# Both sparse layers of a small transformer: norm, router, top two and slots in one block instead of three or four, and attention heads without padding

## The reference

```python
# L1_ffn: 8 experts, two per token
h = (x - mu) * rsqrt(var + 1e-5) * ln_g + ln_b
logits = einsum('btd,ed->bte', h, w_r) + b_r
topk_vals, topk_idx = top_k(logits, 2)
gates = softmax(topk_vals)
mixed = sum(experts(h)[topk_idx] * gates)          # gelu FFN, 128 -> 512 -> 128
# L2_ffn: 8 heads of 16 features
x = x + depthwise_conv3(x) + pos_b
q, k, v = split(x @ qkv_w.T + qkv_b)
idx = top_k(q . k * 128**-0.5, 16);  out = softmax over those 16, times v;  out @ wo_w.T + wo_b
# L3_ffn: 16 experts, two per token, and a shared one
gate_probs = softmax(xf @ gate_w + gate_b);  w, idx = top_k(gate_probs, 2);  w = w / sum(w)
# every expert: swiglu with clamps softplus(raw), scale a[1], shift a[2], then @ expert_w2 + b2
```

## Time and profile before

| what | value |
|---|---|
| median of 3 runs | 1469.47 us (1467.23 to 1474.43) |
| the profiled execution, its own time | 1468.95 us |
| its span in the trace | 1467.1 us |
| busy share PE, DVE, ACT, POOL | 77%, 79%, 45%, 45% |
| first sparse layer, norm to slots | 367.2 to 399.6 us |
| top-16 attention | 621.7 to 1248.4 us |
| state-space block | 1260.4 to 1287.5 us |
| second sparse layer, norm to slots | 1287.8 to 1329.4 us |
| its experts | 1329.7 us to the end |

### The profile page before, as it was taken

How to read it: one execution, slowest core, us unless ns; L and a number is a source line. 1 busy time by engine, 2 the same in 40 slices (tenths; PEclk the granted TensorE clock), 3 DMA queues, 4 the chain that set the end, 5 groups by cost and what they waited for, 6 DMA issues and landing times. The chain is left out here.

```text
span 1467.1 us, 29812 instructions
## 1 busy us (share of the span) xinstructions
PE 1128.4 (77%) x10536; PEld 794.0 (54%) x10544; DVE 1153.9 (79%) x2165; ACT 656.7 (45%) x1184; POOL 656.4 (45%) x569
## 2 busy tenths in 40 slices
PE   5877989998599987888777777777777775758771
PEld 3735566665489966645444444444444444547660
DVE  4676766562625599689999999999999996757994
ACT  4253434342125422156556555655565553013771
POOL 2033324240275762235555555555555554215344
PEclk9899999999689999999999999999999998879995
DMA  4090000000248710000000000000000000003882
GB/s 136 1 269 2 2 2 3 2 2 2 67 135 230 205 37 1 1 1 1 1 0 0 0 0 0 0 0 0 0 0 0 0 1 0 1 7 93 246 248 76
DMA packets 83386, 65.01 MB, mean 44 GB/s; under 512 B 13946, under 2 KB 73748, under 8 KB 83028
## 3 DMA queue, kind: packets, MB, share of 16 engines
q1 hardware_dynamic: 62868, 46.86, 11.4%
q0 software_dynamic: 4096, 8.40, 2.1%
q10 hardware_dynamic: 16320, 8.40, 1.9%
HBM read 43.70 MB, written 22.28 MB: 45 GB/s over the span
## 5 line engine op out<-in xcount | busy, mean ns | idle before, releaser
L1202 POOL TENSOR_TENSOR ta_ex<-ta_ex,ta_left 128x1024 f32<-128x1024 f32 x128 | 301.4, 2355 | 261.1 <-DVE ta_left L1251 261.1
L1071 PE MATMUL ta_ps_t<-consts,ta_ex 128*128 128x128 f32 x1024 | 141.3, 282 | 152.5 <-POOL ta_ex L1202 149.2
L1021 PE MATMUL ta_ps_s<-ta_kT,ta_qz 128*128 (+1 forms) x512 | 245.4, 603 | 0.5 <-ACT ta_ex L1129 0.5
L1071 PEld LDWEIGHTS ta_ps_t<-consts,ta_ex 128*128 128x128 f32 x1024 | 111.4, 142 | 239.0 <-POOL ta_ex L1202 214.3
L1235 DVE MAX8 ta_top<-ta_ps_s 128x8 f32<-128x1024 f32 x128 | 155.9, 1218 | 3.7 <-PE ta_ps_s L1021 3.7
L1241 DVE MATCH_REPLACE8 ta_left<-ta_etop,ta_ex 128x1024 f32<-128x1024 f32 x128 | 154.7, 1209 | 0.0
L1246 DVE MAX8 ta_second<-ta_left 128x8 f32<-128x1024 f32 x128 | 154.7, 1209 | 0.0
L1251 DVE MATCH_REPLACE8 ta_left<-ta_second,ta_left 128x1024 f32<-128x1024 f32 x128 | 154.7, 1208 | 0.0
L1129 ACT ACTIVATE ta_ex<-ta_ps_s,ta_ntop 128x1024 f32<-128x1024 f32 x128 | 140.2, 1096 | 0.0
L1021 PEld LDWEIGHTS ta_ps_s<-ta_kT,ta_qz 128*128 128x128 f32 x512 | 88.9, 192 | 70.5 <-issue 66.8
L2973 ACT ACTIVATE l1h_score<-l1h_work 128x2048 f32<-128x2048 f32 (+1 forms) x40 | 68.5, 1712 | 102.6 <-PE l1h_work L2780 102.5
...
...
## 6 DMA issues: line engine op xcount, KB each, us to landing
...
```

What stands on the lines that cost most here:

```text
L1021: ins = pe.matmul(ps_s[:, i % 2, half * BANK:(half + 1) * BANK], qz[:, odd, h, :], kT[:, grp, bass.ds(at.key0[i // PAIR] + half * BANK, BA ...
L1071: ins = pe.transpose(ps_t[:, j * P:(j + 1) * P], ex[:, i % 4, j * P:(j + 1) * P], m.ident)
L1202: pool.tensor_tensor(ex[:, i % 4, :], ex[:, i % 4, :], left[:, i % 4, :], ALU.subtract).then_inc(kept, 1)
```

## The change

In both sparse layers `routed_norm` takes the place of norm, router and slots: one block, no meeting of the engines inside it. Logits are made group by group (four tiles) into four PSUM banks, between the transposes, whose spins are gone. DVE reads them there: `max` gives a tile's eight largest, `max_index` their positions; the two picks are made from the index (`number` against `m.firsts`), the softmax of two from the difference of the top two values (`gap`), one Exp and a reciprocal. The products of picks with shares (`part`, `r.gates`, `r.scaled`) go to POOL. The rank matrix `later` is `before` minus one, so that the tile's own total need not be subtracted; the scan reads its totals from PSUM, and the rounding takes two operations instead of three. A spin of four matmuls stands ahead of the counting matmuls.

The owner tables (`below`, `owner`) move into the experts' blocks: in the first layer ahead of DVE's first work there, with SP's weight loads and POOL's staging waiting for `owned`; in the second between the first and second `clip`. There the table `par` is split in the shared expert's column (`par_s`, at the start) and the others (`par`, copied at pair 3, from matmuls that PE runs after pair 1 into the bank `ps_x[:, 0]`); the bias matmuls use one bank instead of two; the shares are reduced by DVE after the second `clip`.

The expert scalars move to the beginning of the state-space block (DVE and ACT), and the second layer's parameter DMAs move from its norm to the norm ahead of the state-space block. In the attention the padding is gone: q and k are one group of 128 rows, `m.eighth` masks a head of 16 rows, 4 first and 4 late projections instead of 8 and 8.

PE in the second sparse layer, before: the last rows of the norm, then the router, then the slots (`l3r_ps_l` are the logits, `l3k_ps_t` and `l3k_ps_r` the counts, an UNCONDITIONAL_BRANCH the end or start of a block).

The diff, cut to its core:

```diff
+def routed_norm(nc, m, r, name, E, blocks, wrT, src, dst, dstT, twice=False, fetch=None, gain=None, shift=None, scale=None, warm=0):
...
+            for g in range(TILES // 4):
+                dve.wait_ge(logits, g + 1)
+                for t in range(4 * g, 4 * g + 4):
+                    ins = dve.max(top[:, t, :], banks[g][:, (t % 4) * E:(t % 4 + 1) * E])
+                ins.then_inc(topped, 1)
+                dve.wait_ge(topped, g + 1)
+                for t in range(4 * g, 4 * g + 4):
+                    ins = dve.max_index(index[:, t, :], top[:, t, :], banks[g][:, (t % 4) * E:(t % 4 + 1) * E])
+                ins.then_inc(indexed, 1)
+            dve.wait_ge(indexed, TILES // 4)
+            dve.tensor_scalar(number[:, :, :], index[:, :, 0:2].rearrange("p t k -> p k t"), float(P), None, ALU.mult).then_inc(numbered, 1)
+            dve.tensor_tensor(gap[:, :], top[:, :, 1], top[:, :, 0], ALU.subtract).then_inc(gap_ready, 1)
+            dve.wait_ge(numbered, 1)
+            for k in range(2):
+                dve.tensor_tensor(r.picks[:, k, :, :], ...firsts..., ...number[:, k, :]..., ALU.is_equal).then_inc(picked, 1)
+            dve.wait_ge(picked, 2)
+            dve.tensor_tensor(kept[:, :, :, :], by_expert[0], by_expert[1], ALU.add).then_inc(kept_ready, 1)
+            dve.wait_ge(gap_exp, 1)
...
+            dve.tensor_tensor_scan(flat, again..., ps_t[:, 0:TILES * E], 0.0, ALU.mult, ALU.add).then_inc(step, 1)
+            dve.tensor_scalar(size[:, :, :], cum[:, :, :, CH - 1], (P - 1) / 2.0, CEIL, ALU.add, ALU.add).then_inc(step, 1)
+            dve.tensor_scalar(size[:, :, :], size[:, :, :], CEIL, None, ALU.subtract).then_inc(step, 1)
+            dve.tensor_tensor_scan(r.end..., again_e..., size..., 0.0, ALU.mult, ALU.add).then_inc(step, 1)
+            dve.tensor_tensor(first[:, :, :], r.end[:, :, :], size[:, :, :], ALU.subtract).then_inc(step, 1)
+            dve.tensor_tensor(cum..., cum..., first..., ALU.add).then_inc(step, 1)
+            dve.tensor_tensor(rank..., cum[:, :, :, :], ps_r..., ALU.add).then_inc(step, 1)
+            for k in range(2):
+                ins = dve.tensor_tensor(where[:, k, :, :], r.picks[:, k, :, :], rank[:, :, :], ALU.mult)
+            dve.tensor_reduce(slot[:, :, :], where[:, :, :, :], AX.X, ALU.add).then_inc(step, 1)
+            dve.tensor_copy(r.slot[:, :, :], slot[:, :, :])
 
         @block.gpsimd
+            pool.wait_ge(shared, 1)
+            for k in range(2):
+                pool.tensor_tensor(part[:, k, :, :], r.picks[:, k, :, :], shares[:, k, :]..., ALU.mult).then_inc(weighed, 1)
+            pool.tensor_tensor(r.gates[:, :, 0:E], part[:, 0, :, :], part[:, 1, :, :], ALU.add)
+            if scale is not None:
+                pool.tensor_tensor(r.scaled..., part..., scale..., ALU.mult)
 
         @block.tensor
             spin(pe, m, ps[:, 3, :], 8)
+            for g in range(TILES // 4):
+                for t in range(4 * g, 4 * g + 4):
+                    pe.wait_ge(normed, t + 1)
+                    ins = pe.transpose(ps[:, g, (t % 4) * P:(t % 4 + 1) * P], dst[:, t, :], m.ident)
+                ins.then_inc(turned, 1)
+                if g >= 1:
+                    score(g - 1)
+            score(TILES // 4 - 1)
+            spin(pe, m, ps[:, 0, :], 4)
+            pe.wait_ge(kept_ready, 1)
+            pe.matmul(ps_t[:, 0:TILES * E], m.one, kept..., start=True, stop=True).then_inc(ranked, 1)
+            pe.matmul(ps_r[:, 0:TILES * E], m.later, kept..., start=True, stop=True).then_inc(ranked, 1)
+            spin(pe, m, ps[:, 1, :], warm)
...
 def ssm_run  (@block.vector, ahead of the four jobs; ACT runs Exp, Ln and a priming Exp)
+            dve.scalar_tensor_tensor(size, raw, -1.0, raw, ALU.mult, ALU.max).then_inc(par_step, 1)
+            dve.wait_ge(par_exp, 2)
+            dve.scalar_tensor_tensor(clamp, raw, 0.0, soft, ALU.max, ALU.add).then_inc(par_step, 1)
...
+            dve.tensor_copy(x.wide[:, :, :], one[:, :].unsqueeze(2).broadcast_to([G, 6, L3_I]))
...
 def l3_experts  (@block.tensor)
+                if j == 1:
+                    pe.wait_ge(hot_step, 1)
+                    limits(ps_x[:, 0, :], hot[:, :], COLS)
 (@block.vector)
             clip(0)
+            dve.tensor_tensor(below..., r.end..., m.firsts..., ALU.is_le).then_inc(own_step, 1)
+            dve.tensor_reduce(owner[:, :, :], below[:, :, :, :], AX.X, ALU.add).then_inc(own_step, 1)
...
             clip(1)
+            dve.tensor_reduce(share[:, :, :], r.scaled[:, :, :, :], AX.X, ALU.add).then_inc(share_step, 1)
             for j in range(PAIRS):
+                if j == 3:
+                    dve.wait_ge(par_ready, 2)
+                    dve.tensor_copy(par..., ps_x[0:L3_I, 0, 0:7 * COLS]).then_inc(par_in, 1)
...
 def topk_attend
-            for k in range(4, 8):
-                pe.wait_ge(proj_done, k - 3)
-                project_first(k)
```

More of the change, by code:

```diff
@@ L850, in stage_l1_ffn @@
         r.gates = sb("gates", [P, TILES, 8])
-        r.picks, r.share = sb("picks", [P, 2, TILES, 8]), sb("share", [P, 2, TILES])
+        r.picks, r.shares = sb("picks", [P, 2, TILES, 8]), sb("shares", [P, 2, TILES])
+        r.end = sb("end", [P, B, 8])
         r.slot, r.owner = sb("slot", [P, 2, TILES], I32), sb("owner", [P, B, L1_BLOCKS], I32)
@@ L1404, in stage_l3_ffn @@
         r.hT, r.gates = m.xnT, sb("gates", [P, TILES, G])
-        r.picks, r.share = sb("picks", [P, 2, TILES, L3_E]), sb("share", [P, 2, TILES])
-        r.slot, r.owner = sb("slot", [P, 2, TILES], I32), sb("owner", [P, B, L3_BLOCKS], I32)
+        r.picks, r.shares, r.scaled = sb("picks", [P, 2, TILES, L3_E]), sb("shares", [P, 2, TILES]), sb("scaled", [P, 2, TILES, L3_E])
+        r.slot, r.end, r.hot_s = sb("slot", [P, 2, TILES], I32), sb("end", [P, B, L3_E]), sb("hot_s", [G, 1])
         r.gate_w, r.b_r = sb("gate_w", [P, L3_E]), sb("b_r", [1, L3_E])
@@ new lines, in _ @@
+            dve.wait_ge(picked, 2)
+            by_expert = [r.picks[:, k, :, :].rearrange("p (b t) e -> p b e t", b=B) for k in range(2)]
+            dve.tensor_tensor(kept[:, :, :, :], by_expert[0], by_expert[1], ALU.add).then_inc(kept_ready, 1)
+            dve.wait_ge(gap_exp, 1)
+            dve.tensor_scalar(shares[:, 0, :], gap[:, :], 1.0, None, ALU.add).then_inc(summed, 1)
+            dve.wait_ge(summed, 1)
+            dve.reciprocal(shares[:, 0, :], shares[:, 0, :]).then_inc(summed, 1)
@@ new lines, in _ @@
+            dve.wait_ge(summed, 2)
+            dve.tensor_tensor(shares[:, 1, :], gap[:, :], shares[:, 0, :], ALU.mult).then_inc(shared, 1)
+            if twice:
+                for k, of in enumerate(halves):
+                    dve.tensor_tensor(r.lift[:, 1, of], mean[:, of], rates[:, k, 1, :], ALU.mult)
+                    dve.tensor_scalar(r.lift[:, 0, of], rates[:, k, 1, :], 1.0, None, ALU.add)
+            dve.wait_ge(resets, 4)
+            dve.wait_ge(ranked, 1)
+            dve.nop(nofuse=True)
@@ L2014, in _, with score @@
-            for t in range(TILES):
-                pe.wait_ge(normed, t + 1)
-                ins = pe.transpose(ps[:, t // 4, (t % 4) * P:(t % 4 + 1) * P], r.hn[:, t, :], m.ident)
-                if t % 4 == 3:
-                    ins.then_inc(turned, 1)
-                    if t < TILES - 4:
-                        spin(pe, m, ps[:, 3, :], 1)
+            def score(g):
+                pe.matmul(banks[g][:, 0:4 * E].rearrange("p (t e) -> p t e", e=E), m.one[0:1, :],
+                          r.b_r[:, :].unsqueeze(1).broadcast_to([1, 4, E]), start=True, stop=False)
+                pe.wait_ge(hT_in, g + 1)
+                for t in range(4 * g, 4 * g + 4):
+                    ins = pe.matmul(banks[g][:, (t % 4) * E:(t % 4 + 1) * E], dstT[:, t * P:(t + 1) * P], wrT, start=False, stop=(t % 4 == 3))
+                ins.then_inc(logits, 1)
@@ L2022, in _ @@
+            pe.wait_ge(kept_ready, 1)
+            pe.matmul(ps_t[:, 0:TILES * E], m.one, kept[:, :, :, :].rearrange("p b e t -> p (b e t)"), start=True, stop=True).then_inc(ranked, 1)
+            pe.matmul(ps_r[:, 0:TILES * E], m.later, kept[:, :, :, :].rearrange("p b e t -> p (b e t)"), start=True, stop=True).then_inc(ranked, 1)
+            spin(pe, m, ps[:, 1, :], warm)
         @block.scalar
@@ L2079, in l1_experts_l2_attn @@
         prime = sb("prime", [P, 1])
+        below, owner = sb("below", [P, B, NB, E]), sb("owner", [P, B, NB])
         rows_dram = r.rows_dram
```

508 lines of the change are left out of this document (208 added, 300 removed).

## The result

| | before | changed |
|---|---|---|
| median | 1469.63 us (4 runs, 1467.23 to 1474.43) | 1456.35 us (4 runs, 1452.56 to 1459.37) |
| profiled execution (span) | 1468.95 us (1467.1) | 1459.37 us (1457.6) |
| mean granted clock of PE | 0.943 | 0.934 |

The ratio is 0.9895, 95% interval 0.9867 to 0.9923: faster by 13.3 us, where 24 were forecast. 1456.35 lies outside the range of 1440 to 1452. Among the experiments' executions two ran much slower at a low mean clock (one of e5's, 1544.73 us at .73, and one of before's, 1512.15 us at .82), and the ratios and e5's median leave them out. Each entry is the start of one instruction after less its start before; the step is the difference to the entry above.

What follows compares the result with a forecast made beforehand. Norm to slots in both sparse layers was taken as a chain of PE, DVE and ACT taking turns. Terms -8.3 - 2.8 + 1.3 - 14.5 + .5 = -23.8 from 1468.95 gave 1445.15, hence 1445.5 us; range 1440 to 1452.

Steps and rivals of the forecast that it cites:

- Experts of layer 2: Second sparse layer's experts: added owner, table, share-reduction and limit work mostly fits idle time; net +.5 us, bounds -.5 to +3.5.
- Rival B: Granted clock stays low at layer 2's spins (+1.5), attention startup (+1) and state-space back-projection (+1); 1449 us, chance .20.
- The last sign of the prediction: If blocks shorten as said but the total does not, the gain is handed back in the experts, by weights or bank.
- Rival W: Experiments' rival: work added to the shared expert's pairs makes them slow whatever the clock, 1456 us each time; no chance given.
- C: Second layer's experts pay all: limits, single bias bank, share reduction and copy uncovered, +3.5 for +.5; 1448.5 us, chance .15.
- Layer 1, -8.3: First sparse layer, norm to slots: slots there at 391.3 instead of 399.58, -8.3 us.
- Top-16 start, -2.8: Start of top-16 attention: four projections go behind the startup and DVE's first idle shrinks, -2.8 us.
- State space, +1.3: State-space block: expert scalars ahead of job 0 delay z by 1.1; +1.3 us, bounds 0 and +3.1.
- Layer 2, -14.5: Second sparse layer, norm to slots: block ends at 1314.9 instead of 1329.39, -14.5 us; alternatives -13.0 and -16.5.
- The race of spins and DVE: End of layer 2's slots: PE's last spin and DVE's cast end within .5 us of one another.
- Rival E: MAX and MAX_INDEX in both sparse layers cost the same on few elements; at 1.22 each 1507 us, chance .03.
- rival D: More gained: last scores at full clock, DVE not blocked so spins end earlier (-1.5), startup -3.1; 1441 us, chance .12.

Runs made afterwards that it cites:

- e5: e2 with 12 spins instead of 8 at the head of the second sparse layer's norm: median 1450.29 us, ratio .9855 to the kernel before.
- e2: Changed kernel plus four spins in PE's wait ahead of the first expert pair's down: median 1452.62 us, ratio .9875 to the kernel before.
- e1: The changed kernel run again without any edit: median 1455.14 us, ratio .9905 to the kernel before.
- e7: e2 with all expert scalars but the first operation moved ahead of the state-space block's last addition: median 1451.55 us, ratio .9876 to the kernel before.
- e10: The edits of e2, e5 and e7 together: median 1449.41 us, ratio .9847 to the kernel before.
- e3: Changed kernel with layer 2's owner table, limits and copies back ahead of the first clip, two bias banks: median 1457.52 us, ratio .9914 to the kernel before.
- e9: Kernel before with only the changed top-16 attention functions and mask: median 1470.00 us, ratio .9996 to the kernel before.
- e4: Changed kernel without the 14 spins at the end of the second layer's slots: median 1460.64 us, ratio .9935 to the kernel before.
- e6: e2 with POOL's products held until DVE's last operation of the slots: 1464.19 us in its one run.
- e8: e2 without the 4 spins ahead of the counting matmuls in both sparse layers: median 1456.68 us, ratio .9905 to the kernel before.
- e11: Changed kernel without the one spin ahead of each up of pairs 3 to 9: median 1456.38 us, ratio .9906 to the kernel before.
- e12: e10 without the one spin ahead of each up of pairs 3 to 9: median 1452.88 us, ratio .988 to the kernel before.

## Why the prediction was wrong

The step that failed is "Experts of layer 2: net +.5, bounds -.5 to +3.5". It priced instructions, in durations that the earlier trace rows and the pairs of before show at a granted clock of 1.00, and its upper bound assumed only that all of them lie uncovered. The stretch from clip 0 to 13 took 8.2 us more instead of 1.0. The instructions cost 1.08 of it (e2, full clock). The clock cost 7.1 more in the first profile and 3.9 in e1's (clip 0 to 13, less e2's). Rival B named the clock, but put it at the spins, the attention's start and the back-projection, and at 3.5 us in sum; no term had the pairs in it, where PE is 100% busy and every matmul counts twice when the clock is halved. The last sign of the prediction came true, the gain was handed back in the experts, but neither by weights nor by a bank. Rival W, my C, is refuted as the cause: with its work in place the pairs are fast when the clock is full (39.4 us in e2, e5, e7 and e10), and with its work taken out the kernel is no faster (e3).

This one step does not explain the whole miss. The median lies 10.9 us over the forecast, and e2, whose profile has the pairs at the full clock, is 17.9 us faster than its before, where 24 were forecast; 1452.62 would still have been just outside the range. The rest is spread over the steps below, and how much the medians owe to the pairs' clock is known only as the 2.5 us between e1 and e2, within overlapping intervals.

By the other steps:

- Layer 1, -8.3: measured -7.4 (6.6 to 8.9 over ten profiles). The order of events was right; the spins at .50 were sized .9 too short.
- Top-16 start, -2.8: the place gained 3.4, of which 2.65 was a wait for ACT that the prediction did not name, so the size is in part luck. As a term of the kernel's time it is not shown: alone it gave .0 with ±2.5 us (e9).
- State space, +1.3: measured +1.6; z moved by 1.08 as said, the rest is the back-projection at the lower clock.
- Layer 2, -14.5: measured -12.6. The race of spins and DVE ended .17 apart, POOL's cost was 1.8 for 1.9. Transposes and bias instructions were sized at .19 and .15, and took .255 and .31 at .50. The upper figure for a transpose (.27) stood in the prediction, but was used in layer 1 alone.
- MAX and MAX_INDEX: .10 to .17 each by the rows, plus .07 to load the values. Rival E is out.
- Nothing was booked for the other stages. They gave back 2.4 between the first scatter and the attention (1.0 in e1's profile), .8 behind it and .8 at the end. Most of the first arose inside layer 1's experts (the owner table, booked at nothing, is not it: the first turn of scattered rows came only .1 later than the scatter). e2's profile (1449.29) shows what the steps come to with the pairs at the full clock: span 1447.6, 19.5 below before.
- Two slips of the working changed nothing: rival D's terms give 1441.7, not 1441, and POOL's .72 for 256 columns doesn't follow from 2.37 for 1024 by proportion (.59), though .73 was measured.

What stays open: what brings a fall about. In before, in e9 and in the four profiles with the bridge and all spins (e2, e5, e7, e10) the pairs had none; in the two of the changed kernel both had; in the five in which spins were taken out or a wait of PE was lengthened (e4, e6, e8, e11, e12) all had; e3's fell ahead of most pairs. That is a pattern over single profiles, not a cause. Idle time just ahead isn't needed: in e8 PE's last gap before the fall of 1328 was .24, and the 4 us ahead of it were 100% busy with 38 matmuls. The Trainium skill ("TensorE: Matmul & The Clock Gate", Part 1) has the clock fall when the array goes idle and a busy one at full speed; for this fall the trace doesn't agree, and the measurement decides. By that rule e8's pairs would have stayed at 3.0 us.
